# Softmax planes moved piece by piece between two images, and four engine lists in a new order

## The reference

```python
# layer 0
ll, lh, hl, hh = four sums and differences of the pixels of each 2x2 block, times 0.5
ll_out = groupnorm(proj @ attention(ll))     # 8 heads of 16, 1024 positions, rows normalised,
                                             # of every row only the 512 largest scores kept
high_out = high + alpha*groupnorm(pw @ silu(groupnorm(conv3x3(high))))   # high = lh, hl, hh: 384 channels
out = x + 0.1 * inverse(ll + ll_out, high_out)
out = out + 0.1 * groupnorm(w2 @ gelu(groupnorm(w1 @ out)))
# layer 1: attention over 4096 positions, rank 16
q, k, v = Wq @ x + bq, Wk @ x + bk, Wv @ x + bv
out = gamma * (Wo @ (softmax(q.T k / 4) v) + bo) + x
```

## Time and profile before

| | us |
|---|---|
| median of 3 runs | 5599.7 (5597.94 to 5604.44) |
| profiled execution | 5598.1 |
| its span | 5596.3 |
| TensorE matmul busy | 4769.4 (85%) |
| VectorE busy | 4622.6 (83%) |
| ScalarE busy | 4266.1 (76%) |
| GpSimd busy | 261.7 (5%) |
| DMA, mean rate | 33 GB/s |

### The profile page before, as it was taken

The page is one execution under the profiler, slowest core; times in us unless marked ns, Lnnn a source line. Parts: engine busy times, 40 slices in busy tenths (PEclk is TensorE's granted clock), DMA queues, the critical chain, the costliest instruction groups (busy, mean ns, idle before and its releaser), DMA issues.

```text
span 5596.3 us, 93339 instructions
## 1 busy us (share of the span) xinstructions
PE 4769.4 (85%) x30180; PEld 3089.7 (55%) x30180; DVE 4622.6 (83%) x9087; ACT 4266.1 (76%) x6779; POOL 261.7 (5%) x125
## 2 busy tenths in 40 slices
PE   4444899988999889988999889998899979997799
PEld 2001366654666446663666546664566636664588
DVE  4888799987999789987999879997899979996553
ACT  3884799948998589966999489985899669995333
POOL 2001000020000200010000200002000100000000
PEclk7555899998999989998999989999899989999899
DMA  1001200012001110012000120011200120001100
GB/s 57 7 11 51 63 15 16 15 57 66 16 20 49 38 48 18 16 61 63 15 16 14 58 66 16 20 44 37 54 16 18 60 64 15 16 13 44 36 12 16
DMA packets 101990, 187.43 MB, mean 33 GB/s; under 512 B 47640, under 2 KB 52664, under 8 KB 95832
## 3 DMA queue, kind: packets, MB, share of 16 engines
q1 hardware_dynamic: 101464, 181.02, 11.2%
HBM read 110.09 MB, written 69.47 MB: 32 GB/s over the span
## 4 chain that ended last, share of the span: by engine, by line
DVE 37%; PE 32%; issue 16%; ACT 7%; DMA 3%; SPq 2%; DVEq 1%; POOL 1%; ACTq 0%; POOLq 0%
PE PS L599 11%; DVE M L1772 8%; DVE MX L1940 8%; PE PS L565 5%; DVE work L1763 5%; PE PS L541 3%; ACT work L1194 3%; DVE work L1755 3%; DVE arena L1869 3%; PE PS L583 3%; PE PS L531 2%; PE PS L463 2%; ACT work L1247 1%; PE PS L1068 1%; PE PS L978 1%
## 5 line engine op out<-in xcount | busy, mean ns | idle before, releaser
L599 PEld LDWEIGHTS PS<-V,work 128*128 128x128 f32 x16384 | 2102.7, 192 | 163.4 <-ACT work L1255 23.0
L599 PE MATMUL PS<-V,work 128*128 128x129 f32 x16384 | 2122.1, 276 | 13.6 <-ACT work L1255 12.3
L1194 ACT ACTIVATE work<-arena,T 128x1024 bf16<-128x1024 f32 x1504 | 1715.5, 1144 | 63.0 <-DVE T L1713 47.8
L1940 DVE TENSOR_REDUCE MX<-PS 128x1 f32<-128x512 f32 x2048 | 1396.5, 686 | 291.9 <-PE PS L565 276.5
L1255 ACT ACTIVATE work<-PS 128x1024 f32<-128x1024 f32 x1024 | 1042.2, 1019 | 314.0 <-PE PS L583 312.1
L565 PE MATMUL PS<-KP,QP 96*128 96x512 bf16 x2048 | 848.3, 416 | 115.2 <-DMA QP<-scr 57.6
L1772 DVE MAX8 M<-work 128x8 f32<-128x512 f32 x1024 | 651.8, 681 | 0.5
L1186 ACT ACTIVATE arena<-PS 128x1024 f32<-128x1024 f32 x512 | 524.3, 1024 | 151.8 <-PE PS L463 142.6
L583 PE MATMUL PS<-QP,KP 99*128 99x512 bf16 x2048 | 620.5, 385 | 22.7 <-ACT work L1255 19.4
L1869 DVE SCALAR_TENSOR_TENSOR arena<-PS,work 128x512 f32<-128x512 f32 x896 | 601.3, 684 | 28.7 <-ACT work L1247 18.4
L1247 ACT ACTIVATE work<-PS 128x512 f32<-128x512 f32 x896 | 514.8, 592 | 112.9 <-PE PS L531 109.6
(11 more groups left out here) (193 smaller groups left out, 4158.2 us busy)
## 6 DMA issues: line engine op xcount, KB each, us to landing
work<-scr SPq DMA_DIRECT2D x752, 32.0 KB, 1.8
work<-in_x SPq DMA_DIRECT2D x16, 1024.0 KB, 6.7
arena<-in_x SPq DMA_DIRECT2D x8, 2048.0 KB, 10.8
scrX<-arena SPq DMA_DIRECT2D x8, 2048.0 KB, 6.7
XR<-scrX SPq DMA_DIRECT2D x64, 256.0 KB, 2.7
out<-YO SPq DMA_DIRECT2D x64, 256.0 KB, 2.1
scr<-work SPq DMA_DIRECT2D x24, 512.0 KB, 2.6
scrL<-work SPq DMA_DIRECT2D x24, 512.0 KB, 8.0
```

The source lines that it names most:

```text
L599: last = mm(PS[:, 5 + i // 2, 136 * (i % 2):136 * (i % 2) + 129], P1[:, (16 * j + k) % 3, t, 128 * i:128 * i + 128], V1[:, mt, :], start=( ...
L1194: A(junk[:, m % 2, :], scores(h, i), ACT.Sign, scale=-1.0, bias=T[:, h % 2, i:i + 1], accum_out=CA[:, h % 2, i:i + 1]).then_inc(s["ca"], 1)
L1940: V.reduce_max(MX[:, c % 2, i, w:w + 1], PS[:, maxbank(c, k, l0), :], AX.X).then_inc(s["mr"], 1)
```

## The change

- Layer 1's planes: the first and second plane are stored as each is made and loaded as soon as its own store has landed, KP1 whole and QP1 in two parts, its first quarter (enough for two chunks) ahead and the rest behind. The third plane isn't stored: `copy_plane1` copies it from PT1 to KP1 and QP1 inside SBUF. `maxima(0, 0)` waits for `qp1` (15 transfers an image), `maxima(2, 0)` for the new `qp2` (8 more).
- Layer 0's planes: each has a semaphore of its own (`scrw`, `scrv`, `scru`). Head 0's six loads of plane 0 are issued before plane 1 is stored, the four of plane 1 after the copies of plane 2.
- ScalarE gets waits before `evict(1, 0)` (`qp1`, `qp2`) and before `l1_exp(0, 0)` (`scru`), since these write over what the transfers read.
- The lists of TensorE, ScalarE and VectorE are in a new order, between images, in `alone`, in `first`, `search` and `closing`. No operation is added or removed. GpSimd's list stays.

The diff's core: SyncE, then TensorE, then ScalarE, then VectorE. Of the reordered lists it shows one part of `search` on TensorE and on ScalarE, and the lists between images.

```diff
+          scrv scru scrw1 scry1 qp1 qp2 v1p v1c m mr mp mt mpt mq st1 e1 pv1 on nt xr0 xr1 y1 out0 out1 dset dimg dpr pimg g1 g2 g3 g4
           g5 gs u1 u2 u3 u4 u5 hs qn ye si de dn bc bw xg xl sth eh ph dld dls kon dc1 dc2 free""".split()
...
                             sp.dma_start(QK0[HD * j:HD * j + HD, h % 3, w, :], scr0[t, d, w, :]).then_inc(done, 16)
 
-            def load_planes(parts):
-                for w, dst in ((1, KP1), (0, QP1)):
-                    for j, pair in enumerate(TERMS):
-                        if pair[w] in parts:
-                            sp.dma_start(dst[HD * j:HD * j + HD], scr1[pair[w], HD * w:HD * w + HD, :]).then_inc(s["qp1"], 16)
-
-            def store_plane(n, t, made):
+            def store_plane1(f, t, made, done):
+                sp.wait_ge(s[made], f + 1)
+                for j in range(4):
+                    sp.dma_start(scr1[t][:, N0 * j:N0 * j + N0], PT1[32 * j:32 * j + 32, t, :]).then_inc(s[done], 16)
+
+            def load_plane1(w, dst, t, cols, done):
+                for j, pair in enumerate(TERMS):
+                    if pair[w] == t:
+                        sp.dma_start(dst[HD * j:HD * j + HD, cols], scr1[t, HD * w:HD * w + HD, cols]).then_inc(s[done], 16)
+
+            def copy_plane1(w, dst, t, parts, done):
+                for j, pair in enumerate(TERMS):
+                    if pair[w] == t:
+                        for i in parts:
+                            sp.dma_start(dst[HD * j:HD * j + HD, N0 * i:N0 * i + N0],
+                                         PT1[32 * i + HD * w:32 * i + HD * w + HD, t, :]).then_inc(s[done], 16)
+
+            def store_plane(n, t, made, done):
                 sp.wait_ge(s[made], (n + 1) * 2)
-                sp.dma_start(scr0[t].rearrange("p w n -> p (w n)"), PT[:, t, :]).then_inc(s["scrw"], 16)
...
-                    store_plane(n, 0, "p0")
-                    store_plane(n, 1, "p1")
+                    store_plane(n, 0, "p0", "scrw")
                     sp.wait_ge(s["vt"], (n + 1) * 2)
                     sp.sem_inc(s["free"], 1)
-                    sp.wait_ge(s["scrw"], n * 48 + 32)
-                    load_head(0, (0, 1))
-                    store_plane(n, 2, "p2")
+                    sp.wait_ge(s["scrw"], (n + 1) * 16)
+                    load_head(0, (0,))
+                    store_plane(n, 1, "p1", "scrv")
+                    store_plane(n, 2, "p2", "scru")
                     head0_late()
+                    sp.wait_ge(s["scrv"], (n + 1) * 16)
+                    load_head(0, (1,))
                 if fin:
-                    for a, made in enumerate(("p10", "p11", "p12")):
-                        sp.wait_ge(s[made], f + 1)
-                        for j in range(4):
-                            sp.dma_start(scr1[a][:, N0 * j:N0 * j + N0], PT1[32 * j:32 * j + 32, a, :])                                .then_inc(s["scrw1" if a < 2 else "scry1"], 16)
-                    sp.wait_ge(s["scrw1"], (f + 1) * 128)
-                    load_planes((0, 1))
+                    store_plane1(f, 0, "p10", "scrw1")
+                    store_plane1(f, 1, "p11", "scry1")
+                    first, rest = slice(0, N0), slice(N0, N1)
+                    sp.wait_ge(s["scrw1"], (f + 1) * 64)
+                    load_plane1(1, KP1, 0, slice(0, N1), "qp1")
                     sp.wait_ge(s["scry1"], (f + 1) * 64)
-                    load_planes((2,))
+                    load_plane1(1, KP1, 1, slice(0, N1), "qp1")
+                    load_plane1(0, QP1, 0, first, "qp1")
+                    load_plane1(0, QP1, 1, first, "qp1")
+                    sp.wait_ge(s["p12"], f + 1)
+                    copy_plane1(1, KP1, 2, range(4), "qp1")
+                    copy_plane1(0, QP1, 2, range(1), "qp1")
+                    load_plane1(0, QP1, 0, rest, "qp2")
+                    load_plane1(0, QP1, 1, rest, "qp2")
+                    copy_plane1(0, QP1, 2, range(1, 4), "qp2")
                 if opn:
-                    sp.wait_ge(s["scrw"], (n + 1) * 48)
+                    sp.wait_ge(s["scru"], (n + 1) * 16)
...
                     if k == 0 and c == 0:
-                        pe.wait_ge(s["qp1"], b * 192)
+                        pe.wait_ge(s["qp1"], b * 240)
                         pe.wait_ge(s["v1c"], b * 8)
+                    if k == 0 and c == 2:
+                        pe.wait_ge(s["qp2"], b * 128)
                     if k == 0 and c >= 2:
                         pe.wait_ge(s["y1"], a * NCH + c + (1 if l0 else 0))
...
                     l1_weigh(h - 1, 5, (1,))
                     l1_weigh(h - 1, 6, (0,))
-                    maxima(h, 12)
-                    l1_score(h - 1, 7)
                     l1_weigh(h - 1, 6, (1,))
+                    found_sum(h - 1)
+                    l1_score(h - 1, 8)
+                    maxima(h, 13)
                     l1_weigh(h - 1, 7, (0,))
-                    found_sum(h - 1)
-                    maxima(h, 13)
-                    l1_weigh(h - 1, 7, (1,))
-                    l1_score(h - 1, 8)
+                    l1_score(h - 1, 9)
                     maxima(h, 14)
                     turn(h - 1)
-                    l1_score(h - 1, 9)
+                    l1_weigh(h - 1, 7, (1,))
...
                 qk0(2)
                 proj(0)
                 proj(1)
+                conv(0, 0, 2)
+                group(0)
                 qk0(3)
-                group(0)
-                conv(0, 0, 2)
                 ungroup(0)
                 squares()
...
                 conv(0, 1, 1)
-                spread(0)
                 group(3)
                 spread(1)
                 ungroup(3)
                 conv(0, 1, 2)
-                spread(2)
                 ffn2(0)
                 ffn2(1)
...
                 ffn2(5)
                 ungroup(1)
+                spread(2)
+                ffn2(6)
                 spread(3)
-                ffn2(6)
                 ffn2(7)
                 points(0, 0)
                 points(0, 1)
+                group(4)
                 points(1, 0)
+                ungroup(4)
                 points(1, 1)
-                group(4)
-                ungroup(4)
                 points(2, 0)
                 points(2, 1)
                 qk1()
                 score0(0)
+                group(2)
+                score0(1)
                 values1(0)
-                score0(1)
+                score0(2)
                 values1(1)
-                score0(2)
+                ungroup(2)
+                score0(3)
                 values1(2)
-                score0(3)
+                values1(3)
                 score0(4)
-                values1(3)
+                values1(4)
+                values1(5)
                 score0(5)
-                group(2)
-                values1(4)
+                values1(6)
                 score0(6)
-                values1(5)
-                ungroup(2)
                 score0(7)
-                values1(6)
                 values1(7)
...
+                        need(act, s["scrw1"], b * 64)
                         need(act, s["scry1"], b * 64)
+                        need(act, s["qp1"], b * 240)
+                        need(act, s["qp2"], b * 128)
                         need(act, s["xs"], b * 16)
                     act.wait_ge(s["S"], (b * NH + h) * NT + i + 1)
                     stored(h, i)
...
+                    if l0 and j == 0 and k == 0:
+                        need(act, s["scru"], (b + 1) * 16)
...
                     count(h, 2, 0)
-                    l1_exp(h - 1, 11)
                     half_e(h - 1, 3, 0)
                     count(h, 2, 1)
                     half_e(h - 1, 3, 1)
-                    l1_exp(h - 1, 12)
-                    half_e(h - 1, 4, 0)
+                    l1_exp(h - 1, 11)
                     count(h, 2, 2)
                     count(h, 2, 3)
+                    half_e(h - 1, 4, 0)
...
                 gelu(1)
                 gelu(2)
                 gelu(3)
+                conv(0, 1)
+                gelu(4)
+                gelu(5)
                 ffn2(0)
-                conv(0, 0)
-                gelu(4)
                 ffn2(1)
-                conv(0, 1)
-                gelu(5)
-                gelu(6)
                 ffn2(2)
                 ffn2(3)
+                gelu(6)
                 gelu(7)
                 ffn2(4)
+                part0(0, 0)
+                silu(0)
                 ffn2(5)
-                silu(0)
                 silu(1)
                 silu(2)
                 ffn2(6)
-                part0(0, 0)
+                part0(0, 1)
+                ffn2(7)
+                points(0, 0)
                 part0(1, 0)
-                points(0, 0)
-                ffn2(7)
-                part0(0, 1)
+                part0(1, 1)
                 points(0, 1)
+                norm2(0)
                 points(1, 0)
-                part0(1, 1)
-                points(1, 1)
```

(85 more changed lines are left out.)

300 lines of the change are left out of this document (151 added, 149 removed).

## The result

The changed kernel takes 5559.5 us (median of 6 runs, 5554.6 to 5561.3) against 5598.9 us for the kernel before (6 runs, 5597.8 to 5604.4): a ratio of 0.9927, 95% interval 0.9915 to 0.9940. That is 39 us where 64 were predicted. The sign is right and 5559.5 lies inside the forecast's own range of 5515 to 5560, but by half a microsecond only: 25 us of the gain are missing, and rival (c)'s 5553 is nearer than the forecast's 5535. The range was met by luck as much as by the sum. The profiled execution took 5560.1 us (span 5558.3), 38.0 us less than that of before.

What follows compares the result with a forecast made beforehand. Heads were nearly packed; between images, planes travelling through DRAM set two places. Gains of 40, 19 and 6.7 us, less 2, plus 0 for the heads, made 64 us: 5535 us, own range 5515 to 5560, 8 in 10 5498 to 5590.

Steps and rivals of the forecast that it cites:

- rival (c): Stage between images: its new lists give nothing, one engine's late operation taking back the gain; 45 us, 5553, chance 0.15.
- Part 1: Between images: layer 1's planes land before V is copied, so first `maxima` follows the last V copy; 40 us over seven images.
- (a): Between images: layer 1's planes still come last, `maxima` gaining 3.6 us on average; 5553 us, chance 0.11.
- (b): Between images: each small plane transfer pays its whole landing, one after another; 61 us slower, 5661, chance 0.02.
- Parts 2 and 3: Between images: head 0's planes and new lists together bring the first eviction 2.7 us earlier, bounds -0.7 and +4.3.
- Part 2: Layer 0's head 0 planes between images: rearranged loads bring the first eviction only about 0.9 us earlier without new lists.
- part 3: New lists between images: first eviction 4.3 us earlier including head 0's planes, less 0.6 us at the stage's head.
- The last stage: Stage with only layer 1 left: last plane copy lands at 5209.8 where the matmul started at 5216.53; gain 6.7 us.
- `dls`: VectorE's `apart(0, 0)` waits about 1 us each in images 3 and 7 for later `scrL` stores; 2 us lost in all.
- Part 4: Reordered lists of the heads, 56 with both layers and 8 alone: taken as 0, range -0.5 to +1.5 us a head.
- rival (d): Heads' lists: `l1_exp(11)` waits behind half exponentials and a count; at 1.5 us a head, 32 us slower, 5630, chance 0.08.
- Rival (e): Heads shorter by 0.5 us, one way being a clock that stays high; 32 us more gain, 5503, chance 0.12.

Runs made afterwards that it cites:

- the planes alone: Kernel before with only layer planes' load order on SyncE, on-chip copies and semaphores changed, all engine lists old: 5550.9 us, ratio to before 0.9915.
- the heads' old lists: Changed kernel with search, closing, alone, first and the join of two heads back in the old order on all three engines: 5543.2 us, ratio to before 0.9906.
- the same lists with new lone heads: Changed kernel with the heads' lists old, but `alone` and TensorE's join of two heads still new: 5545.3 us, ratio to before 0.9902.

## Why the prediction was right, and where it was not

- **Part 1, planes of layer 1: right.** The first `maxima` moved from 5.7 us behind the last V copy to 0.15 us behind it. In the last stage the chain can be followed without cover: I had 14.0 us from the first store to the last copy's landing, and it ran from 5164.17 to 5178.16, 14.0.

```profile
5164.17 4.05 SPq L287 DMA_DIRECT2D scr<-arena  x8
5168.27 2.29 SPq L292 DMA_DIRECT2D KP<-scr  x5
5170.61 2.27 SPq L292 DMA_DIRECT2D QP<-scr  x5
5172.92 2.42 SPq L298 DMA_DIRECT2D KP<-arena  x4
5175.39 0.59 SPq L298 DMA_DIRECT2D QP<-arena  x1
```

```profile
5175.39 2.77 DMA QP<-arena
5178.25 0.60 PE PS L587
```

  The first fence is SyncE's timeline, the second the chain that ended last. Rivals (a) and (b) fell with it. The chain is 20.8 us before, from the earlier trace rows. It has 23 transfers now, ten of them of 32 KB, where it had 24 larger ones, so the small pieces did not make it longer. DMA: Bandwidth & Descriptors, Rules for kernel authors, of the Trainium skill says that transfers under 64 KB pay mostly overhead. The trace agrees for one alone, 2.8 us for 32 KB, and shows that these times overlap: the five copies of the last stage are issued over 3.0 us, and only the last one's landing, 2.8 us, is paid.

- **Parts 2 and 3: right in sum, by luck.** 2.7 us were predicted, the first eviction came 2.1 us sooner and the last V copy 2.8. Parts 1 to 3 together were to bring 59 us over seven stages, and `maxima` came 7 x 8.4 = 59 us sooner. But the split was wrong. Part 2 was to give 0.9 us without the new lists; the planes alone gave 1.5 at the first eviction, 2.6 at the last V copy and 8.2 of the 8.4 us at `maxima`. Beside them the new lists between images added 0.2 us there, where part 3 had 1.8. (Beside the old planes they gave 3.6.) So rival (c), that these lists give nothing, was nearly right at that point; over a whole image they are worth 0.8 to 2.4 us, not settled closer. One reason shows in the V copies: with the planes alone they took 18.6 us from the first eviction in six of seven stages, before, 20.3 in the mean.

- **The last stage: 6.7 us predicted, 3.8 measured from `proj` on.** What was off was to start it from the old 5195.77: from `proj` to the first store it took 70.5 us before and 73.4 after, and 72.5 with the planes alone. So most of the delay comes with the old lists too, and the new order is not shown to be its cause. In this stretch the granted clock was 0.78 before, 0.73 after and 0.74 with the planes alone, and TensorE was busy 42.2, 44.0 and 44.1 us of it, which is most of the difference; each is one execution. From image 7's last threshold to `proj`, on the other hand, the changed kernel is 2.7 us shorter (39.2 instead of 42.0). All nine kernels with the new `closing` are at 38.8 to 40.0 there, all five with the old one at 41.9 to 42.8. From that threshold to `maxima` the changed kernel gained 6.6 us.

- **`dls`: right in size, not in place.** 2 us were predicted, in images 3 and 7, and `apart` waits 2.0 us for `scrL` in the whole execution, in images 1, 4 and 5.

```profile
L1781 DVE TENSOR_SCALAR work<-arena,T 128x1024 f32<-128x1024 f32 x512 | 373.5, 745 | 2.9 <-DMA scrL<-work 2.0
```

- **Part 4, the heads' lists: wrong, and this is the missing gain.** I took 0, with -0.5 to +1.5 us a head as bounds, from one argument for and one against; no row gave either a size. Measured: +0.50 in five spacings, +0.46, +0.84, 3.8 us an image and 27 in all. The direction was rival (d)'s, at half of the size from which it decides. Its mechanism was not shown to be the one: `l1_exp(11)` was what I had named, and the step found is a weighing of TensorE. Rival (e) fell: steady heads ran at full clock in both kernels (1.00 in the earlier trace rows and above) and were longer.

The sum with the measured terms: 59 + 3.8 - 27, + 2 for image 0 (image 1's stage begins at 537.0 instead of 539.1, for which I had 0: the lone heads are 4 us shorter in all, the stretches before and behind them 1 us longer each), - 2.6 for 0.37 us more between `maxima` and the first threshold of seven images (the 2 us of `dls` lie in it), + 2.7 behind image 7's last threshold = 38, which is what lies between the profiled executions.

## What to carry to other kernels

Where three engines run hand-written lists at 93% busy, a list has no price of its own: a change of one step costs or gives nothing, or a third of a microsecond, depending on the other lists, and one list of the old set among the new ones cost up to 9.5 us of 63. So look in each engine's new order for long operations put ahead of something that another packed engine waits for, and multiply by the repetitions: here one line was worth 0.35 us in each of some 40 heads. Look at the single heads and their clock before you trust a mean: a mean that said 0.19 us a head was five long heads in 35. When a change has two parts that touch different stages, measure them apart first; the better kernel was the change without half of it.

## What the runs showed of the hardware

From the first eviction to the last V copy the seven stages of the changed kernel take 18.6 to 18.7 us four times, 19.3 once and 21.5 twice, in the same execution and with the same instructions. Images 3 and 4 of the changed kernel, in windows of 4 us (columns as above):

```profile
1928.00:1932.00 4.00, 2.99 (x25) 0.87 (x24) 2.33 (x9) 2.22 (x3) 0.00 (x0) 1.00 0.01 2
...
1936.00:1940.00 4.00, 4.00 (x17) 3.39 (x17) 1.29 (x4) 2.64 (x6) 0.00 (x0) 0.50 0.73 152
1940.00:1944.00 4.00, 4.00 (x18) 3.57 (x18) 0.50 (x2) 3.15 (x7) 0.00 (x0) 0.50 0.92 116
...
2582.00:2586.00 4.00, 2.55 (x24) 1.05 (x17) 1.13 (x7) 3.20 (x5) 0.00 (x0) 1.00 0.01 2
2586.00:2590.00 4.00, 4.00 (x20) 3.25 (x18) 1.72 (x5) 3.71 (x8) 0.54 (x1) 0.57 0.35 89
2590.00:2594.00 4.00, 4.00 (x33) 3.68 (x34) 1.79 (x5) 3.82 (x9) 0.00 (x0) 1.00 0.95 173
```

In both images TensorE's granted clock falls from 1.00, the 2.4 GHz level, to 0.50, the 1.2 GHz level, soon after a stretch with idle time (it was busy 2.99 of 4 us in image 3's, 2.55 in image 4's). In image 3 it stays there for the 8 us shown, with the engine busy throughout, and TensorE does 35 matmuls in them; in the 8 us shown of image 4 the clock is back at 1.00 after the first 4, and 53 are done. All seven stages agree: the first stretch at the lower level behind the first eviction lasted about 3 us where the copies took 18.6 to 19.3 us, and about 10 us where they took 21.5. ScalarE waits for it, and `maxima` starts at 113.2 in image 3's stage and at 109.4 in image 4's. Before, the same spread was there (18.6 to 22.2 us) but was hidden behind the planes. Now the V copies end last and it goes into the time. In the profiled execution of the heads' old lists (5534.0 us) six of seven stages lie between 18.6 and 19.5 us and one is at 21.5; in that of the same lists with new lone heads (5552.7 us) four are between 21.4 and 21.6. That may be a part of the spread of 17 us, but no experiment tested it, and it can't be all: the kernel before spreads as far (5587.4 to 5603.2 us in 13 runs) and the planes alone by 4 us in four runs. What keeps the clock low longer in one image than in the next stays open.
